# A pre-norm attention and mixture-of-experts layer on one core: five full expert tiles of the first sequence are listed while the last router blocks are still chosen, and the expert stage takes buffers in x's place

## The chip, the cores and the metric

One core of one Trainium2 chip runs the whole layer. The metric is device microseconds. Engines: PE (TensorE, matmul), DVE (VectorE), ACT (ScalarE), POOL (GpSimd), SP (which issues most DMAs); each runs its instructions in program order, and they meet at semaphores.

## The reference

```python
x = x + attn(layernorm(x))                      # (2, 2048, 256), 16 heads, softmax, then a local band is added
n = layernorm(x)
probs = softmax(gelu(n @ rW1 + rb1) @ rW2 + rb2)     # 4 experts
weights, chosen = top_k(probs, 2)
out = sum over chosen e of weights_e * (gelu(n @ We1[e] + be1[e]) @ We2[e] + be2[e])
x = x + out
```

Each of the 4096 tokens goes to two of four experts, so 8192 rows pass through an expert.

## The kernel before

After projections and attention come two functions on one block of engine programs. `route` takes the tokens in 8 blocks of 512 (four to a sequence). Per block PE gathers the attention output and the local band (`heads`), multiplies by Wo (`projection`), DVE adds the residual and normalises (`normalise`), PE transposes, ACT and DVE split the result in two float32r halves (`xT_hi`, `xT_lo`), PE makes the router's hidden layer in three products (`router`, L1219, 24 matmuls), ACT applies Gelu, PE makes the logits (L1227) and transposes them. DVE chooses the two experts (`gate`), ACT takes the exponentials, DVE weighs them. PE counts by small matmuls which slot of its expert's region each token gets (`count_slots`, L1243 to L1248), DVE turns that into row numbers (`give_slots`), and POOL scatters the rows to DRAM, eight indirect DMAs a block (`scatter`, L955). The blocks overlap: the choice for block i-1 is written behind the residual of block i+1. When the last block has its slots, DVE makes the table of tiles (`tabulate`, L1086 to L1109): for each of 19 tiles of 512 rows its first row and its expert.

`experts` runs the 19 tiles. SP loads a tile's rows, weights (two halves of 2 MB) and biases, PE transposes the rows (L1475) and ACT and DVE split them. Then per eighth `m` of the hidden layer: `hidden` (L1492, 6 matmuls), Gelu on ACT (L1392), a split on DVE (L1419, L1421), `output` (L1508, 12 matmuls). `hidden` runs two steps ahead of `output`. POOL gathers the output rows, DVE adds, POOL stores. SP waits for every scatter before it loads any tile (L1318), and tile 1's load for the table. The weights of the first tile are loaded earlier (L933), when `o` and `v` have been read, in whose place they stand.

The order is that of the code: each engine's program is written out, and nothing reorders it.

Of the kernel before, what the change touches and what calls it, by code (L numbers as in the profile page):

```python
# [20 lines left out]
F32 = mybir.dt.float32  # L21
# [8 lines left out]
P = 128  # L30
# [5 lines left out]
BT = 4  # L36
# [36 lines left out]
STEPS = TOKENS // SLOTS - 1  # L73

# [749 lines left out]
def route(nc, ctx, dram, keep, block):  # L824
# [3 lines left out]
    def sem(name):  # L828
# [74 lines left out]
    scattered, residual_out, first_weights, table_ready = (  # L903
        keep[n] for n in ("scattered", "residual_out", "first_weights", "table_ready"))
    CONSTS, SETS = 5, 1 + XROWS
    SCATTERS = PER_TOKEN * BT

    @block.sync
    def _(sp):
# [8 lines left out]
        def store_residual(i):  # L918
            sp.wait_ge(residual, i + 1)
            sp.dma_start(dram["out"].rearrange("(n p) f -> p n f", p=P)[:, i * BT:(i + 1) * BT, :],  # L920
                         x_sb[:, i * BT:(i + 1) * BT, :]).then_inc(residual_out, 16)
# [7 lines left out]
        for i in range(1, BLOCKS):  # L929
# [3 lines left out]
        sp.dma_start(keep["w"][0][:].bitcast(F32), dram["w_split"][0:W_CHUNKS].rearrange("c p s f -> p c s f")  # L933
                     ).then_inc(first_weights, 16)
        store_residual(BLOCKS - 1)

    @block.gpsimd
    def _(pool):
# [25 lines left out]
        for i in range(BLOCKS - 2, BLOCKS):  # L964
            scatter(i)

    @block.scalar
    def _(act):
# [34 lines left out]
        for i in range(3):  # L1003
            stage(i)
            copy_heads(i)
            if i == 1:
                copy_hi(0)
        for i in range(BLOCKS):
# [13 lines left out]
        exponentials(BLOCKS - 1)  # L1022

    @block.vector
    def _(dve):
# [4 lines left out]
        per_tile = [P, MOE_TILES, EXPERTS]  # L1030
# [14 lines left out]
        def gate(i):  # L1045
# [39 lines left out]
        def tabulate():  # L1085
            small(nc.vector.tensor_tensor(count[:], free_slot[:], regions, ALU.subtract))  # L1086
            small(nc.vector.tensor_tensor(over[:], count[:].unsqueeze(2).broadcast_to([P, EXPERTS, STEPS]),
                                          full_tiles.unsqueeze(1).broadcast_to([P, EXPERTS, STEPS]), ALU.is_gt))
            small(nc.vector.tensor_reduce(tiles_of[:], over[:], axis=AXIS.X, op=ALU.add))
            small(nc.vector.tensor_scalar_add(tiles_of[:], tiles_of[:], 1.0))  # L1090
            small(nc.vector.tensor_tensor(earlier[:], before[:, 1], tiles_of[:].unsqueeze(1).broadcast_to(pairwise),
                                          ALU.mult))
            small(nc.vector.tensor_reduce(first_tile[:], earlier[:], axis=AXIS.X, op=ALU.add))
            small(nc.vector.memset(reached[:], 0.0))
            small(nc.vector.tensor_tensor(reached[:, :, 0:EXPERTS], tile_at.unsqueeze(2).broadcast_to(per_tile),
                                          first_tile[:].unsqueeze(1).broadcast_to(per_tile), ALU.is_ge))
            small(nc.vector.tensor_tensor(chosen[:], reached[:, :, 0:EXPERTS], reached[:, :, 1:EXPERTS + 1],
                                          ALU.subtract))
            small(nc.vector.scalar_tensor_tensor(shift_of[:], first_tile[:], -float(SLOTS), regions, ALU.mult, ALU.add))
            small(nc.vector.tensor_tensor(by_expert[:], chosen[:], shift_of[:].unsqueeze(1).broadcast_to(per_tile),  # L1100
                                          ALU.mult))
            small(nc.vector.tensor_reduce(start_of[:], by_expert[:], axis=AXIS.X, op=ALU.add))
            small(nc.vector.tensor_tensor(start_of[:], start_of[:], tile_slots, ALU.add))
            small(nc.vector.tensor_scalar_min(start_of[:], start_of[:], float(EXPERTS * REGION)))
            small(nc.vector.tensor_copy(table[:, 0, :], start_of[:]))
            small(nc.vector.tensor_tensor(by_expert[:], chosen[:], expert_at.unsqueeze(1).broadcast_to(per_tile),
                                          ALU.mult))
            small(nc.vector.tensor_reduce(expert_of[:], by_expert[:], axis=AXIS.X, op=ALU.add))
            nc.vector.tensor_copy(table[:, 1, :], expert_of[:]).then_inc(table_ready, 1)  # L1109
# [28 lines left out]

        normalise(0)
        for i in range(BLOCKS):  # L1140
# [12 lines left out]
        read_logits(BLOCKS - 1)  # L1153
        gate(BLOCKS - 1)
        weigh(BLOCKS - 1)
        give_slots(BLOCKS - 1)
        tabulate()

    @block.tensor
    def _(pe):  # L1160
# [90 lines left out]

        heads(0)
        projection(0)
        heads(1)
        for i in range(BLOCKS):
# [18 lines left out]
def experts(nc, ctx, dram, keep, block):  # L1274
    def sb(name, shape, dt=F32):
        return ctx.enter_context(nc.sbuf_tensor(name, shape, dt))

    def sem(name):
        return ctx.enter_context(nc.semaphore(name))

    LAG, PS_H, H, HALVES = 2, 2, 2, 4
    TURN = 4
    ident, w, chosen, table = (keep[n] for n in ("ident", "w", "chosen", "table"))
    xs = [sb(f"xs{u}", [P, BT, ROW]) for u in range(2)]
    biases = [sb(f"biases{u}", [P, MH + DIM]) for u in range(2)]
    xT = [(sb(f"xT_hi{u}", [P, KD, SLOTS], F32R), sb(f"xT_lo{u}", [P, KD, SLOTS], F32R)) for u in range(2)]
    h = [sb(f"h{c}", [P, SLOTS]) for c in range(H)]
    h_hi = [sb(f"h_hi{c}", [P, SLOTS], F32R) for c in range(HALVES)]
    h_lo = [sb(f"h_lo{c}", [P, SLOTS], F32R) for c in range(HALVES)]
    gates = [sb(f"gates{u}", [P, BT, EXPERTS]) for u in range(2)]  # L1290
    gate = [sb(f"gate{u}", [P, BT]) for u in range(2)]
    token = [sb(f"token{u}", [P, BT], U32) for u in range(2)]
    rows = [sb(f"rows{u}", [P, BT, DIM]) for u in range(2)]
    y = [sb(f"y{u}", [P, BT, DIM]) for u in range(2)]
    psum = ctx.enter_context(nc.psum_tensor("psum_experts", [P, 8, BLOCK], F32))
    ps_h = [psum[:, c, :] for c in range(PS_H)]
    ps_x = psum[:, 2:4, :]
    ps_y = [psum[:, 4 + 2 * u:6 + 2 * u, :] for u in range(2)]

    scattered, residual_out, first_weights, table_ready = (  # L1300
        keep[n] for n in ("scattered", "residual_out", "first_weights", "table_ready"))
    xs_in = [sem(f"xs_in{u}") for u in range(2)]
    biases_in = [sem(f"biases_in{u}") for u in range(2)]
    w1_in = [sem(f"w1_in{u}") for u in range(2)]
    w2_in = [sem(f"w2_in{u}") for u in range(2)]
    x_tr, x_hi, x_lo = sem("x_tr"), sem("x_hi"), sem("x_lo")
    prepared, prep_step = sem("prepared"), sem("prep_step")
    h_ready, gelu_done, hi_ready, lo_ready, h_used = (
        sem(n) for n in ("h_ready", "gelu_done", "h_hi_ready", "h_lo_ready", "h_used"))
    y_read, y_gated, y_summed = (sem(n) for n in ("y_read", "y_gated", "y_summed"))  # L1310
    rows_set, gathered, out_stored = sem("rows_set"), sem("gathered"), sem("out_stored")
    W1 = W_CHUNKS // 2
    SCATTERS = PER_TOKEN * BT * BLOCKS // 2

    @block.sync
    def _(sp):
        for u in range(2):
            sp.wait_ge(scattered[u], 16 * SCATTERS)  # L1318
        for i in range(MOE_TILES):
            u = i % 2  # L1320
            if i == 0:
                start, expert = 0, 0
            else:
                sp.wait_ge(table_ready, 1)
                start = sp.value_load(table[0:1, 0, i:i + 1], min_val=0, max_val=EXPERTS * REGION)
                expert = sp.value_load(table[0:1, 1, i:i + 1], min_val=0, max_val=EXPERTS - 1)
            if i >= 2:
                sp.wait_ge(x_tr, i - 1)
                sp.wait_ge(prepared, i - 1)
            sp.dma_start(xs[u][:], dram["xs"][ds(start, SLOTS), :].rearrange("(t p) f -> p t f", p=P)  # L1330
                         ).then_inc(xs_in[u], 16)
# [315 lines left out]
```

## Time and profile before

| | |
|---|---|
| median of 3 runs | 2113.79 us (2111.5 to 2116.76) |
| profiled execution, own time | 2119.99 us |
| its span | 2118.2 us |
| PE, DVE, ACT, POOL busy | 2015.6, 1645.9, 1400.4, 394.8 us |
| mean granted clock of PE | 0.972 |

Busy time is a sum over stages that differ. Attention fills most of the span; the router stage lies at 1459 to 1654 us, the experts at 1654 to 2118 us. What a change between the last two does is read from that stretch alone. The ends of matmuls are modelled, so a result can be ready later than its row ends.

### The profile page before, as it was taken

To read this page: it belongs to the slowest core of one execution; us is meant where nothing else is said; L and a number is where in the kernel's file an instruction comes from. 1 tells how busy PE (TensorE), PEld (TensorE's weight loads), DVE (VectorE), ACT (ScalarE), POOL (GpSimd) and SP (SyncE) were. 2 spreads that over 40 slices of the span, in tenths; PEclk is the share of its full clock that TensorE was granted. 3 is DMA by queue.
4 is the path that set the end of the run, shared out by engine and by line. 5 is a ranking of instruction groups with operands and counts; after the bars stand their busy time and mean duration, and the time that the engine had idled before them with its cause. 6 is when DMAs were issued, how large, how long until landed. Compare 5 with 4: busy or idle time off the path is not lost. (4 is left out here: it accounts for less than half of the span.)

```text
span 2118.2 us, 48429 instructions
## 1 busy us (share of the span) xinstructions
PE 2015.6 (95%) x16588; PEld 1087.0 (51%) x16588; DVE 1645.9 (78%) x1986; ACT 1400.4 (66%) x2500; POOL 394.8 (19%) x463
## 2 busy tenths in 40 slices
PE   7898999999999999999999999998996699999997
PEld 4442333333333333333333333335875599999996
DVE  6586999999999999999999999960454355565564
ACT  3235888888888888888888888896553222222221
POOL 1252001000100100100100010010245233333333
PEclk9897999999999999999999999999997799999998
DMA  7924434533543543453353354321133576776671
GB/s 260 239 52 89 90 70 86 119 74 75 122 83 70 112 98 70 93 117 70 85 119 75 74 121 84 70 69 30 65 111 140 203 263 234 261 268 247 225 271 49
DMA packets 102075, 267.68 MB, mean 126 GB/s; under 512 B 22878, under 2 KB 45920, under 8 KB 95328
## 3 DMA queue, kind: packets, MB, share of 16 engines
q1 hardware_dynamic: 91632, 241.25, 43.2%
q0 software_dynamic: 10368, 25.45, 3.5%
q8 instruction: 45, 0.74, 0.2%
q14 instruction: 30, 0.25, 0.0%
HBM read 212.87 MB, written 74.20 MB: 136 GB/s over the span
## 5 line engine op out<-in xcount | busy, mean ns | idle before, releaser
L586 DVE TENSOR_REDUCE part_max<-psum_attend 128x1 f32<-128x1024 f32 x1024 | 1241.7, 1222 | 78.5 <-PE psum_attend L708 69.7
L641 ACT ACTIVATE probs<-psum_attend 128x512 f32<-128x512 f32 x2048 | 1110.4, 595 | 156.5 <-PE psum_attend L721 71.4
L721 PE MATMUL psum_attend<-score_q,score_k 50*128 50x512 f32 x2048 | 749.2, 448 | 9.4 <-DMA max_k<-qk_pieces 8.1
L708 PE MATMUL psum_attend<-max_k,max_q 48*128 48x512 f32 x2048 | 739.2, 450 | 8.7 <-PEq L1567 6.4
L733 PE MATMUL psum_attend<-probs,v_ones 128*32 128x256 f32 x8192 | 659.0, 393 | 9.0 <-ACT heads_sb L656 8.6
L721 PEld LDWEIGHTS psum_attend<-score_q,score_k 50*128 50x128 f32 x2048 | 309.4, 186 | 418.8 <-ACT probs L641 396.3
L733 PEld LDWEIGHTS psum_attend<-probs,v_ones 128*32 128x32 f32 x8192 | 162.6, 108 | 378.1 <-issue 200.4
L708 PEld LDWEIGHTS psum_attend<-max_k,max_q 48*128 48x128 f32 x2048 | 297.1, 187 | 22.7 <-issue 14.5
L1392 ACT ACTIVATE h<-psum_experts,biases 128x512 f32<-128x512 f32 x152 | 104.8, 689 | 281.8 <-PE psum_experts L1492 251.4
L1508 PE MATMUL psum_experts<-w,h_hi 128*128 128x256 f32 x1216 | 219.7, 280 | 0.0
L1508 PEld LDWEIGHTS psum_experts<-w,h_hi 128*128 128x128 f32 x1216 | 195.6, 188 | 12.5
L1492 PE MATMUL psum_experts<-xT_hi,w 128*128 128x512 f32 x608 | 192.3, 398 | 2.4 <-DVE xT_lo L1400 2.4
L1419 DVE CAST h_hi<-h 128x512 fp32r<-128x512 f32 x152 | 64.9, 427 | 148.8 <-ACT h L1392 124.3
L1508 PE MATMUL psum_experts<-w,h_lo 128*128 128x256 f32 x608 | 170.0, 280 | 0.0
L1368 POOL DMA_INDIRECT out<-y,token x76 | 77.9, 1025 | 232.4 <-DVE y L1444 215.0
L1508 PEld LDWEIGHTS psum_experts<-w,h_lo 128*128 128x128 f32 x608 | 115.5, 190 | 0.0
L547 POOL CAST shift<-neg_max 128x16 fp32r<-128x16 f32 x31 | 6.1, 198 | 577.3 <-DVE neg_max L594 577.3
L1492 PEld LDWEIGHTS psum_experts<-xT_hi,w 128*128 128x128 f32 x608 | 104.4, 190 | 16.7 <-DVE xT_lo L1400 2.8
L1421 DVE TENSOR_TENSOR h_lo<-h,h_hi 128x512 fp32r<-128x512 f32 x152 | 105.2, 692 | 5.2
L1492 PE MATMUL psum_experts<-xT_lo,w 128*128 128x512 f32 x304 | 95.8, 396 | 0.0
L1363 POOL DMA_INDIRECT rows<-out,token x76 | 78.8, 1037 | 68.1 <-DMA out<-y,token 40.8
L512 POOL COPY v_ones<-v_sb 128x256 f32<-128x256 f32 x32 | 12.7, 398 | 353.4 <-PE psum_attend L733 353.2
(152 smaller groups left out, 1302.0 us busy)
## 6 DMA issues: line engine op xcount, KB each, us to landing
w<-w_split SPq DMA_DIRECT2D x36, 2048.0 KB, 9.1
max_q<-qk_pieces SPq DMA_DIRECT2D x192, 128.0 KB, 7.4
score_k<-qk_pieces SPq DMA_DIRECT2D x192, 128.0 KB, 4.7
xs<-in_pads SPq DMA_DIRECT2D x33, 528.0 KB, 5.7
qk_pieces<-pieces SPq DMA_DIRECT2D x32, 512.0 KB, 4.7
w_split<-w_pair SPq DMA_DIRECT2D x32, 512.0 KB, 6.4
max_k<-qk_pieces SPq DMA_DIRECT2D x192, 64.0 KB, 7.6
score_q<-qk_pieces SPq DMA_DIRECT2D x192, 64.0 KB, 2.2
```

Source lines behind the costliest of these rows:

```text
L586: nc.vector.tensor_reduce(part_max[:, t, p:p + 1], ps_m[p].rearrange("q b f -> q (b f)"), axis=AXIS.X, op=ALU.max).then_inc(m_read, 1)
L641: nc.scalar.activation(probs[kb % 2][:, chunk * BLOCK:(chunk + 1) * BLOCK], bank_of(at), ACT.Exp, scale=float(HD) ** -0.5).then_inc(exp_do ...
L708: last = nc.tensor.matmul(ps_m[p][:, h, :], max_q[u][rows, t * P:(t + 1) * P], max_k[u][rows, p * BLOCK:(p + 1) * BLOCK], start=True, stop ...
L721: nc.tensor.matmul(bank_of(at), score_k[u][rows, kb * P:(kb + 1) * P], score_q[u][rows, part * BLOCK:(part + 1) * BLOCK], start=True, stop ...
L733: last = nc.tensor.matmul(ps_o[QUAD * j:QUAD * (j + 1), at:at + BLOCK // PARTS], v_ones[u][:, kb, :], probs[kb % 2][:, j * BLOCK + at:j * ...
L1363: nc.gpsimd.indirect_dma_start(rows[u][:, t, :], None, dram["out"], bass.IndirectOffsetOnAxis(ap=token[u][:, t:t + 1], axis=0), bounds_che ...
L1368: nc.gpsimd.indirect_dma_start(dram["out"], bass.IndirectOffsetOnAxis(ap=token[u][:, t:t + 1], axis=0), y[u][:, t, :], None, bounds_check= ...
L1392: nc.scalar.activation(h[m % H][:], ps_h[m % PS_H], ACT.Gelu, bias=biases[i % 2][:, m:m + 1]).then_inc(gelu_done, 1)
L1419: nc.vector.tensor_copy(h_hi[m % HALVES][:], h[m % H][:]).then_inc(hi_ready, 1)
L1421: nc.vector.tensor_tensor(h_lo[m % HALVES][:], h[m % H][:], h_hi[m % HALVES][:].bitcast(F32), ALU.subtract).then_inc(lo_ready, 1)
L1492: last = nc.tensor.matmul(ps_h[m % PS_H], w[u][:, 2 * k + m // 4, c, at:at + P], xx[:, k, :], start=j == 0, stop=j == len(terms) - 1)
L1508: last = nc.tensor.matmul(ps_y[u][:, t // 2, (t % 2) * DIM:(t % 2 + 1) * DIM], hs[m % HALVES][:, toks], w[u][:, chunk, c, at:at + DIM], st ...
```

## The change

`route` and `experts` become one function, `route_and_experts`, with one set of semaphores. Its main parts:

- Four blocks put 4096 rows into four regions, so at least five tiles are full by then. DVE lists five full tiles (`list_early`) in the loop's sixth round, and the other 14 (`list_late`) inside the first expert tile. The table is read by SP for every tile, the first included.
- SP loads tile 0 when blocks 0 to 3 have been scattered and stored and the first list stands; tile 1 follows. From tile 5 on it waits for all scatters and the second list.
- PE's transposes of tile 0 stand ahead of the last router block, two `hidden` steps around the last logits, and the last `count_slots` behind tile 0's second `output`. DVE chooses, weighs and places the last block between the steps of tile 0. POOL gathers tile 0's rows ahead of the last scatter.
- Rows, hidden values and biases of the tiles lie where blocks 0 to 3 of `x_sb` were, other buffers in place of the router's; PSUM banks are shared with the router's tensors.

```diff
+EARLY = PER_TOKEN * SEQ // SLOTS - EXPERTS + 1
+LATE = MOE_TILES - EARLY
...
+    x_at = x_sb[:].rearrange("p t f -> p (t f)")
...
+    y = [x_sb[:, HALF * BT:HALF * BT + BT, :], attnT[:].rearrange("p k (a f) -> p (k a) f", f=DIM)]
+    rows = [o_st, v_st]
...
+    LAST_LOGITS, LAST_GATES, LAST_SLOTS, LATE_TABLE = 0, 1, 3, 4
...
         sp.wait_ge(staged, BLOCKS)
-        sp.dma_start(keep["w"][0][:].bitcast(F32), dram["w_split"][0:W_CHUNKS].rearrange("c p s f -> p c s f")
-                     ).then_inc(first_weights, 16)
+        def load_tile(i):
+            u = i % 2
+            if i == 0:
+                sp.wait_ge(residual_out[0], 16 * HALF)
+                sp.wait_ge(table_ready, 1)
+                for parity in range(2):
+                    sp.wait_ge(scattered[parity], 16 * SCATTERS * ROUNDS)
+            elif i == EARLY:
+                sp.wait_ge(table_ready, 2)
+                for parity in range(2):
+                    sp.wait_ge(scattered[parity], 16 * SCATTERS * BLOCKS // 2)
...
+        load_tile(0)
         store_residual(BLOCKS - 1)
+        for i in range(1, MOE_TILES):
+            load_tile(i)
...
+        gather_rows(0)
+        scatter(BLOCKS - 1)
+        store_rows(0)
...
         for i in range(BLOCKS):
+            if i == BLOCKS - 1:
+                split_x(0)
             for m in range(MR):
...
+                gelu(i, m)
+                if i == 0 and m == LAST_GATES:
+                    exponentials(BLOCKS - 1)
...
+        def list_early():
+            count_tiles(full[:], ALU.is_ge)
+            sum_earlier(first_full[:], full[:])
+            list_tiles(first_full[:], 0, EARLY, None)
+            small(nc.vector.tensor_scalar(taken[:], first_full[:], -1.0, float(EARLY), ALU.mult, ALU.add))
+            small(nc.vector.tensor_scalar_max(taken[:], taken[:], 0.0))
+            small(nc.vector.tensor_tensor(taken[:], taken[:], full[:], ALU.min))
...
                 read_logits(i - 1)
+                split_x(0)
+                prepare(0)
             if i >= 1:
-                gate(i - 1)
+                choose(i - 1)
                 weigh(i - 1)
+            if i == HALF + 1:
+                list_early()
         give_slots(BLOCKS - 2)
...
+                elif m == LAST_LOGITS:
+                    read_logits(BLOCKS - 1)
+                elif m == LAST_GATES:
+                    choose(BLOCKS - 1)
+                elif m == LAST_SLOTS:
+                    weigh(BLOCKS - 1)
+                    give_slots(BLOCKS - 1)
+                elif m == LATE_TABLE:
+                    list_late()
...
+            if i == BLOCKS - 1:
+                tile_transposes(0)
             router(i)
         count_slots(BLOCKS - 2)
+        hidden(0, 0)
         router_logits(BLOCKS - 1)
+        hidden(0, 1)
         transpose_logits(BLOCKS - 1)
-        count_slots(BLOCKS - 1)
...
                 output(i, m)
+                if i == 0 and m == LAST_GATES:
+                    count_slots(BLOCKS - 1)
```

The order on DVE at the turn from round 5 to round 6 of the router loop, before (the last step of `weigh(4)`, the low half for block 6, then the slots of block 4):

```order
L1068 TENSOR_TENSOR prob<-prob,top 128x16 [waits gate_step]
L1069 TENSOR_TENSOR xrow<-prob,mask 128x4x4 [waits gate_step]
L1142 TENSOR_TENSOR route_xT_lo<-psum_route,route_xT_hi 128x1024 [waits hi_ready,gate_step]
L1075 TENSOR_TENSOR place<-psum_route,free_slot 128x16 [waits place_ready]
L1077 TENSOR_TENSOR free_slot<-psum_route,free_slot 128x4 [waits gate_step]
```

The same place now; the twenty rows from `count` to the third `taken` are `list_early`:

```order
L1203 TENSOR_TENSOR prob<-prob,top 128x16 [waits gate_step]
L1204 TENSOR_TENSOR xrow<-prob,mask 128x4x4 [waits gate_step]
L1249 TENSOR_TENSOR count<-free_slot,numbers 128x4 [waits gate_step]
L1250 TENSOR_TENSOR over<-count,numbers 128x28 [waits gate_step]
...
L1241 CAST table<-expert_of 128x5 [waits gate_step]
L1259 TENSOR_SCALAR taken<-first_full 128x4
L1260 TENSOR_SCALAR taken<-taken 128x4 [waits gate_step]
L1261 TENSOR_TENSOR taken<-taken,full 128x4 [waits gate_step]
L1351 TENSOR_TENSOR route_xT_lo<-psum_route,route_xT_hi 128x1024 [waits hi_ready,gate_step]
L1210 TENSOR_TENSOR place<-psum_route,free_slot 128x16 [waits place_ready]
```

The low half that PE's router matmuls of block 6 wait for now stands behind twenty more instructions of DVE.

PE behind the last router matmuls, now (`w_end` holds the high half of tile 0's rows, `rh` the router's hidden layer; before, the logits of L1461 followed the counting at once, and transposes, the last counting and only then the tile's transposes came after):

```order
L1482 MATMUL psum_route<-mask,counting 128x4 x4
L1509 MATMUL psum_route<-w_end,w 128x512 x2
L1509 MATMUL psum_route<-xT_lo,w 128x512 x2
L1509 MATMUL psum_route<-w_end,w 128x512 x2
L1461 MATMUL psum_route<-rh,w_r 32x512 x4
L1509 MATMUL psum_route<-w_end,w 128x512 x2
L1509 MATMUL psum_route<-xT_lo,w 128x512 x2
L1509 MATMUL psum_route<-w_end,w 128x512 x2
L1468 MATMUL psum_route<-ident_sb,logitsT 128x128 x4
L1509 MATMUL psum_route<-w_end,w 128x512 x2
```

Three `hidden` steps of tile 0 now stand around the last block's logits.

SP at the end of the router loop, now (before, the 4 MB of weights stood first, without a table, and waited for `staged` alone):

```order
L962 DMA out<-x_sb 128x4x256 [waits residual]
L987 TENSOR_LOAD table [waits scattered0,table_ready,scattered1,residual_out0,staged]
L987 ISA x2
L988 TENSOR_LOAD table
L988 ISA x2
L992 ISA
L992 DMA x_sb<-xs 128x4x264
L996 ISA
L996 DMA w<-w_split 128x4x1024
```

Tile 0's rows are now behind the first list, and its weights behind its rows.

## Rows read from the trace of the kernel before

**Rows 1.** Chain of waits, 1616 to 1672 us: start, duration, what

```profile
1601.24 52.92 issue
...
1654.21 3.80 DMA xs<-xs
...
1658.05 1.98 PE psum_experts L1475 x8
...
1662.39 6.69 PE psum_experts L1492 x18
1669.08 1.39 PE psum_experts L1508 x12
```

**Rows 2.** Busy time by stretch: PE, weight loads, DVE, ACT, POOL, clock, DMA, GB/s

```profile
1592.00:1598.00 6.00, 6.00 (x40) 5.25 (x36) 1.16 (x5) 3.71 (x5) 1.92 (x2) 1.00 1.03 420
...
1613.00:1619.00 6.00, 5.07 (x11) 3.57 (x12) 3.69 (x16) 0.69 (x1) 2.70 (x3) 0.50 0.18 68
...
1635.00:1658.00 23.00, 3.58 (x16) 3.49 (x16) 5.24 (x29) 0.00 (x0) 15.31 (x16) 0.50 0.35 119
...
1695.00:1717.95 22.95, 22.95 (x152) 20.88 (x151) 13.63 (x24) 6.39 (x9) 8.12 (x8) 1.00 0.70 249
```

**Rows 3.** Timeline of PE: start, duration, line, operation, count, idle time before

```profile
1592.26 0.40 PE L1243 MATMUL psum_route<-mask,counting 128*128 128x16 f32 x2
...
1594.07 3.70 PE L1191 MATMUL psum_route<-w_o,attnT 128*128 128x256 f32 x16
...
1598.82 0.72 PE L1219 MATMUL psum_route<-route_xT_hi,w_r_hi 128*128 128x512 f32 x2 [0.61 <-DVE route_xT_lo L1142]
...
1603.06 0.72 PE L1219 MATMUL psum_route<-route_xT_hi,w_r_hi 128*128 128x512 f32 x2 [2.58 <-DVE logits L1042]
...
1607.36 1.03 PE L1202 MATMUL psum_route<-ident_sb,xrow 128*128 128x128 f32 x8
...
1613.85 1.22 PE L1219 MATMUL psum_route<-route_xT_hi,w_r_hi 128*128 128x512 f32 x2 [2.03 <-DVE route_xT_lo L1142]
...
1622.25 0.29 PE L1243 MATMUL psum_route<-mask,counting 128*128 128x16 f32 x2
```

**Rows 4.** Timeline of DVE

```profile
1597.54 1.22 DVE L1142 TENSOR_TENSOR route_xT_lo<-psum_route,route_xT_hi 128x1024 fp32r<-128x1024 f32 x1
...
1599.61 1.22 DVE L1115 TENSOR_TENSOR x_sb<-psum_route,x_sb 128x1024 f32<-128x1024 f32 x1
...
1632.35 0.22 DVE L1042 TENSOR_REDUCE logits<-psum_route 128x16 f32<-128x64 f32 x1
...
1639.63 0.15 DVE L1086 TENSOR_TENSOR count<-free_slot,numbers 128x4 f32<-128x4 f32 x1
...
1643.62 0.18 DVE L1109 CAST table<-expert_of 128x19 int32<-128x19 f32 x1
```

**Rows 5.** Timeline of ACT

```profile
1628.35 0.60 ACT L1016 ACTIVATE logitsT<-psum_route 128x512 f32<-128x512 f32 x1 [5.22 <-remote]
1628.97 1.28 ACT L1001 ACT_TABLE_LOAD   x1
1630.26 0.22 ACT L1001 ACTIVATE prob<-below_top 128x16 f32<-128x16 f32 x1
```

**Rows 6.** Costliest groups: busy, mean ns of one, idle before

```profile
L1392 ACT ACTIVATE h<-psum_experts,biases 128x512 f32<-128x512 f32 x152 | 104.8, 689 | 281.8 <-PE psum_experts L1492 251.4
L1419 DVE CAST h_hi<-h 128x512 fp32r<-128x512 f32 x152 | 64.9, 427 | 148.8 <-ACT h L1392 124.3
L1421 DVE TENSOR_TENSOR h_lo<-h,h_hi 128x512 fp32r<-128x512 f32 x152 | 105.2, 692 | 5.2
```

**Rows 7.** Timeline of SP, tile 0's biases and tile 1's rows

```profile
1654.62 0.51 SPq L1346 DMA_DIRECT2D biases<-in_be  x1
1656.75 0.39 SPq L1330 DMA_DIRECT2D xs<-xs  x1
```

**Rows 8.** Timeline of POOL, the last indirect DMA of block 3

```profile
1593.55 0.96 POOL L955 DMA_INDIRECT xs<-xrow,slot_at  x1 [0.30 <-issue]
```

More of the change, by code:

```diff
@@ L821, in _, with route_and_experts @@
         transpose_heads(ps_tr).then_inc(last_tr, 1)
-def route(nc, ctx, dram, keep, block):
+def route_and_experts(nc, ctx, dram, keep, block):
     def sb(name, shape, dt=F32):
@@ new lines, in route_and_experts @@
+    LAG, PS_H, H, HALVES = 2, 2, 2, 4
+    TURN = 4
+    w = keep["w"]
+    x_at = x_sb[:].rearrange("p t f -> p (t f)")
+    ends = np.cumsum([0, BT * ROW, BT * ROW, SLOTS, SLOTS, MH + DIM, MH + DIM])
+    xs0, xs1, h0, h1, biases0, biases1 = (x_at[:, int(a):int(b)] for a, b in zip(ends, ends[1:]))
+    xs = [part.rearrange("p (t f) -> p t f", f=ROW) for part in (xs0, xs1)]
+    h, biases = [h0, h1], [biases0, biases1]
+    y = [x_sb[:, HALF * BT:HALF * BT + BT, :], attnT[:].rearrange("p k (a f) -> p (k a) f", f=DIM)]
@@ new lines, in route_and_experts @@
+    full = sb("full", [P, EXPERTS])
+    first_full = sb("first_full", [P, EXPERTS])
+    taken = sb("taken", [P, EXPERTS])
+    ps_x = psum[:, 2:4, :]
+    ps_h = [psum[:, 4 + c, :] for c in range(PS_H)]
+    ps_y = [psum[:, 6:8, :], psum[:, 0:2, :]]
+    xs_in = [sem(f"xs_in{u}") for u in range(2)]
+    biases_in = [sem(f"biases_in{u}") for u in range(2)]
+    w1_in = [sem(f"w1_in{u}") for u in range(2)]
+    w2_in = [sem(f"w2_in{u}") for u in range(2)]
+    x_tr, x_hi, x_lo = sem("x_tr"), sem("x_hi"), sem("x_lo")
@@ L1021, in _, with gelu @@
                 copy_heads(i + 3)
-        exponentials(BLOCKS - 1)
+        def gelu(i, m):
+            s = MH * i + m
+            act.wait_ge(h_ready, s + 1)
+            if s < H:
+                act.wait_ge(residual_out[0], 16 * HALF)
+            else:
+                act.wait_ge(h_lo_ready, s - H + 1)
+            nc.scalar.activation(h[m % H], ps_h[m % PS_H], ACT.Gelu, bias=biases[i % 2][:, m:m + 1]
+                                 ).then_inc(gelu_done, 1)
+        for i in range(MOE_TILES):
+            act.wait_ge(biases_in[i % 2], 16 * (i // 2 + 1))
+            for m in range(MH):
+                if m == TURN + LAG and i + 1 < MOE_TILES:
+                    split_x(i + 1)
+                gelu(i, m)
+                if i == 0 and m == LAST_GATES:
+                    exponentials(BLOCKS - 1)
     @block.vector
@@ L1250, in count_slots, with tile_transposes, hidden, output @@
             last.then_inc(place_ready, 1)
+        def tile_transposes(i):
+            u = i % 2
+            pe.wait_ge(xs_in[u], 16 * (i // 2 + 1))
+            if i == 0:
+                pe.wait_ge(residual, BLOCKS)
+            else:
+                pe.wait_ge(x_lo, i)
+            for k in range(KD):
+                for t in range(BT):
+                    last = nc.tensor.transpose(ps_x[:, k, t * P:(t + 1) * P], xs[u][:, t, k * P:(k + 1) * P], ident[:])
+            last.then_inc(x_tr, 1)
+        def hidden(i, m):
+            u, s = i % 2, MH * i + m
+            if m == 0:
+                pe.wait_ge(x_lo, i + 1)
+                pe.wait_ge(w1_in[u], 16 * (i // 2 + 1))
+            if s >= PS_H:
+                pe.wait_ge(gelu_done, s - PS_H + 1)
+            hi, lo = xT[u]
+            at = (m % 4) * P
+            terms = [(c, xx, k) for c, xx in ((0, hi), (0, lo), (1, hi)) for k in range(KD)]
+            for j, (c, xx, k) in enumerate(terms):
+                last = nc.tensor.matmul(ps_h[m % PS_H], w[u][:, 2 * k + m // 4, c, at:at + P], xx[:, k, :],
+                                        start=j == 0, stop=j == len(terms) - 1)
+            last.then_inc(h_ready, 1)
+        def output(i, m):
+            u, s = i % 2, MH * i + m
+            if m == 0:
+                pe.wait_ge(w2_in[u], 16 * (i // 2 + 1))
+                if i == 0:
+                    pe.wait_ge(lg_read, BLOCKS)
+                elif i == 1:
+                    pe.wait_ge(place_read, BLOCKS)
+                else:
+                    pe.wait_ge(y_read, i - 1)
+            pe.wait_ge(h_lo_ready, s + 1)
+            chunk, at = W1 + m // 2, (m % 2) * DIM
+            for t in range(BT):
+                toks = slice(t * P, (t + 1) * P)
+                for j, (hs, c) in enumerate(((h_hi, 0), (h_hi, 1), (h_lo, 0))):
+                    last = nc.tensor.matmul(ps_y[u][:, t // 2, (t % 2) * DIM:(t % 2 + 1) * DIM],
+                                            hs[m % HALVES][:, toks], w[u][:, chunk, c, at:at + DIM],
+                                            start=m == 0 and j == 0 and t % 2 == 0,
+                                            stop=m == MH - 1 and j == 2 and t % 2 == 1)
+            last.then_inc(h_used, 1)
         heads(0)
@@ L1519, in _ @@
                 if m == TURN and i + 1 < MOE_TILES:
-                    transposes(i + 1)
+                    tile_transposes(i + 1)
                 if m + LAG < MH:
@@ L1571, in program @@
             keep["w"] = [token_sb(f"w{u}", [P, W_CHUNKS, 2, CHUNK], F32R) for u in range(2)]
-            token_sb("o_end", [P, NHEADS * (ST + 2) * HD + (NHEADS + 1) * ST * HD - 4 * W_CHUNKS * CHUNK])
-            with nc.Block() as block:
-                for stage in (route, experts):
-                    with ExitStack() as ctx:
-                        stage(nc, ctx, dram, keep, block)
+            keep["w_end"] = token_sb("w_end", [P, NHEADS * (ST + 2) * HD + (NHEADS + 1) * ST * HD - 4 * W_CHUNKS * CHUNK], F32R)
+            with nc.Block() as block, ExitStack() as ctx:
+                route_and_experts(nc, ctx, dram, keep, block)
 def local_band():
```

435 lines of the change are left out of this document (172 added, 263 removed).

## The prediction

> **What bounds the kernel now.** I read the page's slices first: PE is busy nearly everywhere, with one hole between the router stage and the experts. The chain of waits shows what the hole is made of [rows 1]: from 1601.24 us it follows no engine for 52.92 us, until tile 0's rows are fetched at 1654.21; transposes, the split and six-matmul `hidden` steps follow, and the first `output` starts at 1669.08. From there PE runs without a gap: a tile's stretch shows PE busy for all of its 22.95 us, at full clock, with DVE busy for 13.63 and ACT for 6.39 [rows 2]. So whatever makes the first `output` start earlier moves the end by as much, unless a tile gets longer. In the 23 us before the fetch PE is busy for 3.58 [rows 2]; SP waits there for POOL's last scatters, and nothing of the experts is allowed to begin.
>
> Three smaller waits inside the router matter, because the change adds to them. In block 6 PE's router matmuls start 0.61 us late, on DVE's low half, and wait 2.58 us more for the logits of block 5; in block 7 they wait 2.03 us for the low half [rows 3]. DVE has no pause ahead of the first of these: the low half at 1597.54 follows the weighing directly [rows 4]. That DVE chain is on the path.
>
> **What goes.** All of the serial tail: the last count, placing, table, last 16 scatter issues, fetch, transposes and split with PE idle. I do not count it as a difference of idle times but rebuild the new start of the first `output`, in the old clock, from the end of the last router matmul at 1622.25 [rows 3].
>
> - Before, ACT could copy the last logits at 1628.35 [rows 5], 6.10 us after that matmul; a count of slots and the logits lie between. Now one `hidden` step lies there too: 18 such matmuls took 4.30 us at full clock, from 1603.06 to 1607.36 [rows 3], so six take 1.43. Logits are copied from 1629.8.
> - ACT must then copy (0.60), load the exponential's table (1.28), take block 6's exponentials (0.22) [rows 5], load Gelu's table (1.28 again) and run the first Gelu (0.69) [rows 6]: 4.1 us, to 1633.9. PE fills part of this with the second `hidden` step and the transposes of the logits, then waits about 2 us for that Gelu.
> - DVE splits it (0.43 and 0.69 [rows 6]) and reads the logits (0.22 [rows 4]), which free the PSUM banks that `output` writes: 1.4 us with the gaps. The first `output` can start at 1635.4.
>
> That is 33.7 us before 1669.08, and the same three `hidden` steps lie ahead of it in both kernels. The last counting is now PE work behind this point; in the stream one count takes 1594.07 - 1592.26 = 1.8 us [rows 3]. Left: 31.9 us.
>
> **What it costs.** The first list is twenty DVE instructions that each wait for the one before, straight in the chain that PE waits for in block 6. The old table's eighteen stand at a pitch of (1643.62 - 1639.63)/17 = 0.235 us, and the shortest lasts 0.15 [rows 4]: 3.0 to 4.7 us. Their operands are smaller now, 5 tiles for 19, so I take 0.21 each: 4.2 us, all of it on the path, since residual, transposes and low half of block 7 follow in the same program. Nothing later in the router absorbs it: block 7 waits for DVE too.
>
> PE then idles about 4.8 us instead of 0.61 ahead of block 6's router matmuls, and 2.6 again behind the first six. Clock: in block 7 of the old kernel PE had waited 2.03 us, and the stretch from 1613 ran at a granted 0.50, the 1.2 GHz level [rows 2, 3]; likewise the first 18 expert matmuls, after the long wait, took 6.69 us [rows 1] where 18 take 4.30 at full clock. So a fall costs 2.4 us per 18 matmuls. I charge it once for block 6; bounds are 0 and 4.8 (if its transposes and logits run slow too). Block 7's own loss is in the old times already: 24 matmuls from 1613.85 to 1622.25, 8.4 us for 5.7 [rows 3]; the 2.7 may go, as tile 0's transposes now fill that wait.
>
> The Trainium skill speaks against the change here ("TensorE: Matmul & The Clock Gate", Part 1: the throttled state is the default and activity releases it). The trace agrees with it at 1613; by that rule alone both blocks would run at the lower level, which is the upper bound just given.
>
> Around the first logits of tile 0, PE's work is broken by the 2 us wait, so some first steps may run at the lower level: 0 to 2.4 us by the same price, 1.4 taken.
>
> DVE in tile 0 carries choosing, weighing, placing and the second list, some 40 instructions at 0.235 = 9.4 us. Of a normal tile's 13.63 us three additions on the output (1.22 each, as the 128x1024 low half [rows 4]) do not exist yet. 10.0 + 9.4 is under 22.95, and `hidden` runs two steps ahead of `output`, so I cost it at nothing; in the worst place, the choice (12 instructions, 2.8 us) and two tables on ACT (2.6 us) could stall PE by up to 3 us once.
>
> SP: the first list stands at about 1601.1, reading table entries takes 1656.75 - 1654.62 - 0.51 = 1.6 us [rows 7], the fetch 3.8 [rows 1]: rows at 1606.5. PE wants them behind the transposed logits of block 6, about 1616 with the shift. Covered by 9 us. Block 3's scatter was issued by 1594.5 [rows 8], so it is not what SP waits for. First weights: rows and 2.1 MB at the 420 GB/s of [rows 2] are 6 us, at 1609 to 1610, wanted about 1628. Tile 0's other weights and biases need 2.2 MB more, 5 us; the store of block 7's residual and tile 1's loads queue behind, and their first reader is PE in the middle of tile 0. POOL's four gathers ahead of the last scatter cost it about 5 us (0.96 + 0.30 each [rows 8]); the last scatter has until tile 5's load, three tiles later. The other 14 tiles keep their work, and the tail is unchanged.
>
> These loads now run beside POOL's scatters. While 4 MB of weights moved at 420 GB/s [rows 2], POOL issued its indirect DMAs at 0.96 + 0.30 us as ever [rows 8]. The Trainium skill warns that transfers from SP and POOL share the same 16 engines and interleave ("DMA: Bandwidth & Descriptors", Issuing engines are not separate DMA queues). If that halved SP's rate, rows and first weights would be there by 1616 still, so the sum stays.
>
> Sum: 31.9 - 4.2 - 2.4 - 1.4 = 23.9 us. The profiled execution took 2119.99, so it would be 2096.1; it lies 6.2 above the median of 2113.79, and against that the forecast is 2090. Best case: 31.9 - 3.0 + 2.7 = 31.6, 2082. Worst of the same mechanism: 31.9 - 4.7 - 4.8 - 2.4 - 3.0 = 17, 2097.
>
> **Rivals.**
>
> *The clock and the stalls eat more.* If PE stays at the lower level from block 6 to tile 0's first steps, block 6 loses 4.8, the logits and counts behind it some 3 (a count alone is 1.8 at full clock), and tile 0's first 36 matmuls 4.8, with a list of 4.7 and a stall of 3: the gain is 31.9 - 20 = 12, 2102. For it: four short waits of PE in a row. Against: from 1603 to 1607 it ran at full speed right behind a wait of 2.58 us [rows 3].
>
> *Tile 0's rows come late.* Its transposes stand in PE's program ahead of the last router block, so each us late is a us lost. If the rows landed only with everything behind them in SP's queue (two tiles' rows, weights and biases and a residual block, 10.3 MB at 420 GB/s, 24 us, 1627), PE would lose 11 more: gain 13, 2101. Against it: 3.8 us for the same fetch [rows 1].
>
> *The change doesn't begin early.* If the first weights came only behind all scatters, the hole would stay: 2114, perhaps 2118 with the list. Nothing in the waits asks for that.
>
> *Slower: the buffers in x's place.* Rows, hidden values, biases and one output share the area of `x_sb`. If DVE's or ACT's accesses there ran slower, each tile would stretch once DVE passes PE's 22.95 us: from 13.63 that needs a factor of 1.7. At double, 27.3 a tile, 19 tiles lose 83 us: 2173. It decides the sign from 1.3 us a tile on (24/19). Against: DVE's addition into `x_sb` takes the same 1.22 us for 128x1024 as the split into another buffer [rows 4].
>
> **Chances.** Forecast with its bounds (2082 to 2097): 0.66. Clock and stalls (2097 to 2107): 0.15. Late rows: 0.07. More gain than my best case, if the exposed part of the list is smaller: 0.04. No effect: 0.05. Slower: 0.03. Range 2081 to 2103: it takes in both middle rivals. Measurements of this kernel tell about 0.3%, 6.3 us, from no change; faster by more: 0.92, within: 0.05, slower: 0.03.
>
> **What would show it.** From the last router matmul to the first `output` it is 46.8 us in the old trace (1669.08 - 1622.25); about 14.6 would be right, with PE waits near 2 us instead of the hole. Twenty DVE rows ahead of block 6's low half, and PE idle there near 5 us with a lower clock behind. Tile 0's transposes inside block 7's wait, without a pause on a DMA. Tiles still at 23 us. Wrong if PE waits for `xs` or `w`, if a tile grows by 1 us, or if block 6's router is not delayed by the list.

## The result, and the profile after

The changed kernel takes 2094.91 us, median of 4 runs (2084.94 to 2116.38), against 2112.64 in the same job: ratio 0.9887, 95% interval 0.9839 to 0.9936. The slowest of the four was disturbed and is left out of the ratio. Forecast: 2090, 2081 to 2103. The two profiled executions took 2119.99 and 2096.47: 23.5 us, where the sum had 23.9. The same kernel timed once more in another job (first experiment) gave 0.9851, 0.9827 to 0.9876.

PE's timeline of the changed kernel, its waits from block 6 to tile 1 and the rows that the text reads, others left out (it answers to [rows 3]; L1453 router, L1468 transposed logits, L1509 `hidden`, L1528 `output`):

```profile
1603.25 1.22 PE L1453 MATMUL psum_route<-route_xT_hi,w_r_hi 128*128 128x512 f32 x2 [4.43 <-DVE route_xT_lo L1351]
1607.49 1.22 PE L1453 MATMUL psum_route<-route_xT_hi,w_r_hi 128*128 128x512 f32 x2 [1.31 <-DVE logits L1177]
1620.18 0.72 PE L1453 MATMUL psum_route<-route_xT_hi,w_r_hi 128*128 128x512 f32 x2 [1.15 <-DVE route_xT_lo L1351]
1626.17 0.29 PE L1477 MATMUL psum_route<-mask,counting 128*128 128x16 f32 x2
1633.48 0.66 PE L1468 MATMUL psum_route<-ident_sb,logitsT 128*128 128x128 f32 x4 [1.41 <-ACT logitsT L1134]
1637.01 1.22 PE L1509 MATMUL psum_route<-w_end,w 128*128 128x512 f32 x2 [2.87 <-ACT x_sb L1148]
1639.73 0.63 PE L1528 MATMUL psum_route<-w,h_hi 128*128 128x256 f32 x2
1645.99 1.03 PE L1482 MATMUL psum_route<-mask,counting 128*128 128x4 f32 x8
1649.95 0.38 PE L1528 MATMUL psum_route<-w,h_hi 128*128 128x256 f32 x1 [0.27 <-issue]
1651.38 0.62 PE L1509 MATMUL psum_route<-xT_lo,w 128*128 128x512 f32 x2 [0.45 <-issue]
1661.63 0.50 PE L1528 MATMUL psum_route<-w,h_hi 128*128 128x256 f32 x2 [1.26 <-DVE h_lo L1321]
```

The hole of [rows 1] is gone: from the end of the last router matmuls (the next row starts at 1626.17) to the first `output` it is 13.56 us, 46.8 before. No pause on rows or weights is left; the longest waits are 4.43 us in block 6, on DVE, and 2.87 ahead of the first `output`.

Stretches of the changed kernel, as [rows 2]: block 6's router, tile 0, a steady tile.

```profile
1602.00:1610.00 8.00, 5.44 (x12) 3.85 (x13) 6.76 (x24) 0.69 (x1) 2.20 (x2) 0.50 0.69 228
1639.73:1670.11 30.38, 27.53 (x169) 24.16 (x168) 17.04 (x59) 7.82 (x11) 17.73 (x18) 0.96 0.45 154
1749.21:1772.31 23.10, 23.10 (x154) 20.92 (x153) 13.76 (x24) 6.55 (x9) 8.10 (x9) 1.00 0.71 257
```

Tile 0 takes 30.38 us for 23.10. The last count is 1.7 of the difference (1645.18 to 1646.88) and the low clock of its first steps (0.50 until 1642) about 1.1; some 4.4 us are new. They lie where two engines wait for PE, which has long finished. DVE's and ACT's timelines of the changed kernel, place and Gelu:

```profile
1654.36 0.18 DVE L1210 TENSOR_TENSOR place<-psum_route,free_slot 128x16 f32<-128x16 f32 x1 [7.45 <-remote]
```
```profile
1654.36 1.27 ACT L1148 ACTIVATE x_sb<-psum_route,x_sb 128x512 f32<-128x512 f32 x2 [9.42 <-remote]
```

The count ended at 1647.02, yet `place`, which needs nothing else, starts at 1654.36, in the same instant as a Gelu that had waited 9.42 us. "remote" says that the trace names no releaser. Ends of matmuls are modelled, so a late signal and a late result look alike here; PE's later matmuls, at any rate, start from 1646.88 on. On POOL twelve indirect transfers stand without a break from 1637.19 to 1652.5 (first and last here):

```profile
1637.19 1.06 POOL L1032 DMA_INDIRECT xs<-xrow,slot_at  x1 [6.03 <-DVE slot_at L1218]
...
1651.51 1.00 POOL L1054 DMA_INDIRECT o_st<-out,token  x1 [0.30 <-issue]
```

### The profile page after: what moved, and what is told of

Read it like the earlier page. It is cut to its first block and busy times, and to the rows that moved or that the text cites. A ratio compares the mean times of both kernels' runs of the same rounds, so it can differ in the third digit from the quotient of the medians.

```text
span 2094.7 us, 48471 instructions
## 1 busy us (share of the span) xinstructions
PE 2024.2 (97%) x16588; PEld 1083.5 (52%) x16588; DVE 1647.9 (79%) x2007; ACT 1402.4 (67%) x2502; POOL 392.9 (19%) x461
## 5 line engine op out<-in xcount | busy, mean ns | idle before, releaser
L1148 ACT ACTIVATE x_sb<-psum_route,x_sb 128x512 f32<-128x512 f32 x152 | 104.5, 689 | 287.0 <-PE psum_route L1509 243.8
L1528 PE MATMUL psum_route<-w,h_hi 128*128 128x256 f32 x1216 | 218.5, 279 | 2.4 <-DVE h_lo L1321 1.3
L1528 PEld LDWEIGHTS psum_route<-w,h_hi 128*128 128x128 f32 x1216 | 195.8, 189 | 16.6 <-issue 1.7
L1319 DVE CAST h_hi<-x_sb 128x512 fp32r<-128x512 f32 x152 | 65.3, 430 | 132.8 <-ACT x_sb L1148 115.3
L1528 PE MATMUL psum_route<-w,h_lo 128*128 128x256 f32 x608 | 169.3, 278 | 0.0
L1528 PEld LDWEIGHTS psum_route<-w,h_lo 128*128 128x128 f32 x608 | 114.7, 189 | 0.2 <-issue 0.2
L1321 DVE TENSOR_TENSOR h_lo<-x_sb,h_hi 128x512 fp32r<-128x512 f32 x152 | 105.4, 693 | 5.2
L1509 PE MATMUL psum_route<-w_end,w 128*128 128x512 f32 x320 | 102.3, 401 | 2.9 <-ACT x_sb L1148 2.9
L1509 PE MATMUL psum_route<-route_xT_hi,w 128*128 128x512 f32 x288 | 91.6, 399 | 0.0
L1032 POOL DMA_INDIRECT xs<-xrow,slot_at x64 | 62.9, 984 | 29.9 <-issue 18.1
```

The source lines that it names most:

```text
L1032: nc.gpsimd.indirect_dma_start(dram["xs"], bass.IndirectOffsetOnAxis(ap=at, axis=0), xrow[i % XROWS][:, t, :], None).then_inc(scattered[i ...
L1148: nc.scalar.activation(h[m % H], ps_h[m % PS_H], ACT.Gelu, bias=biases[i % 2][:, m:m + 1]).then_inc(gelu_done, 1)
L1319: nc.vector.tensor_copy(h_hi[m % HALVES], h[m % H]).then_inc(h_hi_ready, 1)
L1321: nc.vector.tensor_tensor(h_lo[m % HALVES], h[m % H], h_hi[m % HALVES].bitcast(F32), ALU.subtract).then_inc(h_lo_ready, 1)
L1509: last = nc.tensor.matmul(ps_h[m % PS_H], w[u][:, 2 * k + m // 4, c, at:at + P], xx[:, k, :], start=j == 0, stop=j == len(terms) - 1)
L1528: last = nc.tensor.matmul(ps_y[u][:, t // 2, (t % 2) * DIM:(t % 2 + 1) * DIM], hs[m % HALVES][:, toks], w[u][:, chunk, c, at:at + DIM], st ...
```

## The experiments

Stages are compared in us from block 0's first output projection in each profiled execution (1471.34 before, 1472.15 after). That matmul starts anywhere from 1461.9 to 1483.4 in the fourteen executions, behind instructions that no edit touches (buffers lie elsewhere in three of them): so single times say little and the stages more. The stages vary too: the nine executions that have the early list in its place reach block 6's router at 127.5 to 132.1. All are start times of rows; "place" is the time from the last count's end to `place`.

| kernel | router 6 | first `output` | place | tile 0 | end of `output` | ratio to before, interval |
|---|---|---|---|---|---|---|
| before | 127.5 | 197.6 | 0.1 | 23.0 | 632.5 | |
| changed | 131.1 | 167.6 | 7.3 | 30.4 | 608.4 | 0.9887, 0.9839-0.9936 |
| again | 131.7 | 168.5 | 7.9 | 32.5 | 611.5 | 0.9851, 0.9827-0.9876 |
| list hidden | 129.7 | 166.3 | 7.9 | 31.9 | 608.7 | 0.9875, 0.9847-0.9904 |
| gather last | 130.6 | 167.3 | 2.8 | 30.2 | 608.0 | 0.9887, 0.9861-0.9913 |
| late slots | 132.1 | 168.5 | moved | 31.3 | 610.7 | 0.9878, 0.9852-0.9904 |
| few scatters | 131.2 | 164.2 | 0.1 | 26.1 | 600.8 | 0.9843, 0.9802-0.9884 |
| late weights | 127.5 | 163.9 | 6.9 | 38.9 | 613.3 | 0.9882, 0.9830-0.9934 |
| scatters later | 129.5 | 163.7 | 0.1 | 25.8 | 606.9 | 0.9882, 0.9848-0.9915 |
| list hidden, scatters later | 127.9 | 163.6 | 0.1 | 26.9 | 616.4 | 0.9899, 0.9859-0.9939 |
| later, same places | 128.9 | 162.1 | 0.1 | 38.7 | 613.5 | 0.9916, 0.9887-0.9945 |
| list hidden, later, same places | 126.4 | 160.6 | 0.1 | 36.3 | 609.8 | 0.9900, 0.9865-0.9936 |
| shifted by 64 bytes | 129.5 | 166.0 | 7.6 | 30.4 | 613.7 | 0.9917, 0.9885-0.9948 |
| short runs | 127.7 | 160.8 | 0.6 | 25.1 | 599.7 | 0.9844, 0.9810-0.9877 |

**The changed kernel again.** No edit.

> The changed kernel itself, once more. Two theories of what ate 4 of the 29.35 us by which the first `output` comes earlier are told apart by the kernels beside it. Hold: what TensorE signals after the count of the last block and after hidden(0,4) reaches VectorE and ScalarE only when the gather of tile 0's rows on POOL has landed (7.2 us after the matmuls' end in the profiled run). Queue: VectorE's work for the last block stands between the halves of tile 0 and delays them. Both expect here 2090 to 2100 us, a ratio of 0.987 to 0.992 to the kernel before, and again a wait of VectorE's `place` of 5 to 8 us that no engine's work explains.

Tile 0 took 2.1 us more than the first time: behind the same stall the clock fell to 0.57 from 1650 to 1658. The stall repeats; whether it costs clock does not. The ratio, 0.9851, lies just below what was expected.

**The list hidden.**

```diff
                 choose(i - 1)
+                if i == HALF + 1:
+                    list_early()
                 weigh(i - 1)
-            if i == HALF + 1:
-                list_early()
```

> The early list is put between the choosing and the weighing of block 4, where VectorE waited some 8 us for the exponentials. If the list's 4.0 us stand on the path and bring the low clock behind them (18 router matmuls 6.2 us for 4.3), as the prediction has it: VectorE's low half of block 6 follows at once, the wait of 4.4 us on TensorE is gone, the router of block 6 runs at full clock, and the time is 5 to 6 us less than the changed kernel's (2089 to 2091, ratio 0.986). Rival: something else (the scatter of block 3, the last block's rows) is late next and takes the place of the list: the wait changes its name and the time falls by 1 us or less.

Block 6's router began 2.0 us earlier than in the repeated kernel, not 4, and the end of `output` shows no gain. DVE's timeline here:

```profile
1600.12 0.17 DVE L1201 TENSOR_REDUCE top<-prob 128x4 f32<-128x16 f32 x1 [5.71 <-ACT prob L1109]
...
1600.95 1.22 DVE L1351 TENSOR_TENSOR route_xT_lo<-psum_route,route_xT_hi 128x1024 fp32r<-128x1024 f32 x1
```

The list is wholly hidden (it ends at 1594.4), but now the exponentials are late: ACT's copy ahead of them waited 3.39 us with no releaser named and started at 1596.40, where POOL's eight transfers of block 3 had ended at 1596.39. That speaks for the rival, but how much of the gain went there one pair does not tell: the four kernels with the list hidden have block 6's router at 126.4 to 129.7, on average 2.3 us earlier than the nine with it in its place.

**Who holds the signals?**

```diff
-        gather_rows(0)          # gather last
         scatter(BLOCKS - 1)
+        gather_rows(0)
```
```diff
-    ... LAST_SLOTS, LATE_TABLE = 0, 1, 3, 4    # late slots
+    ... LAST_SLOTS, LATE_TABLE = 0, 1, 5, 6
```

> POOL gathers tile 0's rows behind the last block's scatter and not ahead of it, so that nothing of POOL's is under way when TensorE has counted the last block. Hold: VectorE's `place` starts within 1 us of the count's end (7.2 us in the changed kernel), hidden(0,4)'s GELU comes at once, the gaps of TensorE between 1649 and 1663 shrink from 4 us to about 1, and the time falls by 2 to 4 us, to 2091 to 2093. Queue: `place` and the GELU wait as before for what TensorE does, the gaps stay, and the time stays within 1 us (or rises, if the gathered rows now come late for the sum of tile 0).

> Weighing and slots of the last block are moved behind the halves of hidden(0,5), the late list behind those of hidden(0,6); POOL's order is as in the changed kernel. Queue: the halves of hidden(0,4) and hidden(0,5) no longer wait behind `place` and the list, TensorE's gaps of 4 us go, and the time falls by 3 to 4 us. Hold: the signal of hidden(0,4) is still held until the gather has landed, so the GELU of hidden(0,4) is as late as before; the gaps shrink by 1 us at most and the time falls by 0 to 1 us.

With the gather last, `place` came 2.8 us after the count, at 1646.65, 1.1 us behind the last transfer of block 6's scatter (1644.60 + 0.96), for 7.3. But tile 0 stayed at 30.2: the run of transfers, now 1647.95 to 1663.7, stalls PE's next steps instead (0.4 to 0.7 us "issue" each, 1658 to 1662). With DVE's late work moved, a Gelu still waited 10.67 us, until 1.9 us behind the end of POOL's twelve transfers, and tile 0 took 31.3. The queue theory falls; the hold follows POOL.

**Transfers or loads?** Few scatters issues `at = slot_at[i % 2][:, 0:1]` alone for blocks 4 to 7, so that the rows that the other seven carry are missing, and the waits count the fewer scatters. Late weights:

```diff
+            if i == 1:
+                sp.wait_ge(place_read, BLOCKS)
```

> POOL issues one of the eight scatters of each of the blocks 4 to 7 and leaves out the other seven, so those blocks' rows are missing from the late tiles; the first five tiles have all their rows. Hold (what TensorE signals is held while POOL's indirect transfers are under way): TensorE's signals after the logits of blocks 6 and 7, after the count of block 7 and after hidden(0,4) come within 0.5 us of the matmuls' end; from the first output projection of block 0 to tile 1's first `output` it takes 6 to 9 us less than in the changed kernel (198.0 and 201.0 us in its two profiled runs). Rival, the loads: what holds the signals is tile 0's and tile 1's rows and weights at some 420 GB/s, which are all still loaded; the waits stay as they are and the stretch stays within 2 us.

> Tile 1's weights are asked for only when the last block's `place` has been read (some 1654 us), so that between the landing of tile 0's weights and there only POOL's transfers are under way. Loads: `place` comes within 1 us of the count's end (7.2 and 8.1 us in the changed kernel), the GELU of hidden(0,4) is on time. Hold by POOL: `place` still comes 6 to 8 us after the count, at the end of the gather. Either way hidden(1,0) now waits 1 to 4 us for weights that take some 10 us, so the time itself says little here.

DVE's `place` with few scatters, and then with late weights:

```profile
1644.05 0.17 DVE L1215 TENSOR_TENSOR place<-psum_route,free_slot 128x16 f32<-128x16 f32 x1 [0.54 <-PE psum_route L1487]
```
```profile
1639.12 0.17 DVE L1212 TENSOR_TENSOR place<-psum_route,free_slot 128x16 f32<-128x16 f32 x1 [7.27 <-issue]
```

With few scatters tile 0 is 26.1 us (23.1, the count, and 1.3 of low clock) and PE has no gap in it; tile 1 begins 7.6 and 10.7 us earlier than in the changed kernel's two executions. With late weights SP issues nothing from 1593.43 to 1639.67, and `place`, due at 1632.2, is still 6.9 us late; from 1612 to 1639.6 POOL's transfers are all that moves but for two packets of instructions. PE has gaps without a releaser from 1637 to 1652 (up to 1.4 us each), the first two begun before SP's next load; then the clock falls (0.50 from 1652 to 1656), and tile 0 takes 38.9. So it is POOL's transfers, not the loads.

**Moving them.** Blocks 5 to 7 get slot buffers of their own (four in all).

```diff
-        scatter(BLOCKS - 2)
...
         gather_rows(0)
-        scatter(BLOCKS - 1)
+        pool.wait_ge(slot_ready, BLOCKS)
+        scatter(HALF + 1)
         store_rows(0)
         for i in range(1, MOE_TILES):
             gather_rows(i)
+            if i < 3:
+                scatter(HALF + 1 + i)
```

> The scatters of the blocks 5, 6 and 7 are moved out of the way: block 5's behind the last block's slots (four slot buffers in place of two), block 6's behind the gather of tile 1's rows, block 7's behind that of tile 2's; all work is kept. Hold: the last block's signals come at once, `place` follows the count within 1 us, TensorE's idle time and its low clock in tile 0 go in part; tile 1's first `output` comes 4 to 7 us earlier than in the changed kernel, and the time falls by as much, if the scatters hold nothing in the steady tiles. Rival: the moved scatters hold TensorE's signals where they now stand, in tiles 0 to 2, and give 3 to 5 us back there; the time is within 2 us of the changed kernel's.

> The early list in VectorE's wait for block 4's exponentials and the three late scatters moved, both at once. If the list is worth 2 us there (as between the two runs of before), and the scatters 4 to 7, the time is 6 to 9 us below the changed kernel's, 2083 to 2087 where that makes 2092. If the list's gain was lost to a hold of block 3's scatter, which stays, and the moved scatters give back what they win, it is within 2 us of the changed kernel's.

Tile 1 began 8.5 and 11.5 us earlier with the scatters later, but from there each tile took 23.45 us for 23.09 and the end won only 1.5 and 4.6. With both edits tiles 2 and 3 took 25.7 and 29.8 as well: there twelve transfers (four gathers, eight scatters) and then sixteen (four stores more) stand without a break, and PE has gaps of 0.3 to 0.9 us towards the end of both. The kernel with the scatters later has the same two runs there, no gap, and tiles of 23.45 and 23.58: such a run does not always cost. For the pace there is another suspect, the places of buffers, which the extra slot buffers had moved:

```diff
-    slot_at = [sb(f"slot_at{u}", ...) for u in range(4)]
+    slot_at = [sb(f"slot_at{u}", ...) for u in range(2)]    # the other two behind all buffers
```
```diff
+    unused = sb("unused", [P, 2 * PER_TOKEN * BT], U32)     # shifted: the changed kernel and this
```

In the first two of these three, block 6's scatter follows block 5's at once and block 7's stands behind the gather of tile 1.

> The scatters of the blocks 5 and 6 behind the last block's slots, that of block 7 behind the gather of tile 1's rows, so that no scatter stands right before a store of rows; and the two extra slot buffers stand behind all other buffers in SBUF, so that the halves h_hi and h_lo lie where they lie in the changed kernel. Where the buffers lie is what cost 0.36 us a tile in the kernel with the scatters later: then the tiles take 23.1 us again, what the scatters gain (8 us at tile 1) stays to the end, and the time is 6 to 9 us below the changed kernel's of the same chip. Rival: the scatters themselves or the later stores slow each tile: the pitch stays at 23.45 us and the time is 2 us below the changed kernel's or less.

> The same with the early list in VectorE's wait for block 4's exponentials. The list is worth 2 us at block 6's router in both earlier kernels that had it so: 8 to 11 us below the changed kernel's. Rival: a longer hold in another place takes the 2 us, and it is within 1 us of the kernel with the scatters alone.

> The changed kernel with one unused buffer of 64 bytes a partition where the two extra slot buffers stood, so that all buffers behind it lie 64 bytes further; no instruction is another. If where the buffers lie sets the pace of the `output` matmuls: a tile takes 23.45 us for 23.09 (119 ns a matmul for 115), and the time is 6 to 7 us above the changed kernel's, with the stages ahead of the tiles as they were. Rival: the pace came from what the scatters' kernel did otherwise; then the tiles take 23.09 us and the time is that of the changed kernel, 2092 to 2097.

A steady tile by stretch in the shifted kernel (for the changed one's 23.10 see above):

```profile
1832.70:1856.15 23.45, 23.45 (x154) 21.32 (x153) 13.84 (x24) 6.53 (x9) 8.31 (x8) 1.00 0.70 253
```

The places explain the pace: 23.1 with the buffers back, 23.45 from the shift alone. But sixteen scatters in a row made tile 0 38.7 and 36.3 us, and tile 2, beside twelve transfers, took 25.3 and 25.5, so neither kernel won what was expected. PE's timeline in the first of these:

```profile
1659.95 0.39 PE L1513 MATMUL psum_route<-route_xT_hi,w 128*128 128x512 f32 x1 [0.71 <-issue]
1660.67 0.48 PE L1513 MATMUL psum_route<-route_xT_hi,w 128*128 128x512 f32 x1 [0.34 <-issue]
1662.75 0.37 PE L1532 MATMUL psum_route<-w,h_hi 128*128 128x256 f32 x1 [1.59 <-issue]
...
1668.38 0.37 PE L1532 MATMUL psum_route<-w,h_lo 128*128 128x256 f32 x1 [1.73 <-issue]
```

PE stops between matmuls of one step, waiting for nothing that the trace shows, until the run of transfers ends at 1667.2; then comes the low clock (0.53 over 1667 to 1676).

**Short runs.** The previous version with the list hidden, and

```diff
+        pool.wait_ge(h_used, 6)
+        scatter(HALF + 2, [0])                  # four transfers
...
+            if i == 1:
+                scatter(HALF + 2, [1])
+            elif i in (2, 3):
+                scatter(HALF + 3, [i - 2])
```

> The early list hidden, the buffers where they were, and POOL's late scatters cut into runs with pauses between: block 5's eight behind the last block's slots, four of block 6's after six of tile 0's eight steps, four behind each of the gathers of tiles 1, 2 and 3. If what stops TensorE is the length of an unbroken run of POOL's indirect transfers (twelve in the changed kernel's tile 0, sixteen in the kernel with the scatters later, where a tile of 23 us took 38.7 and 36.3), then tile 0 takes 25 to 27 us for 30.4 to 32.5, no tile behind it over 23.6, and the end of the output matmuls, counted from block 0's output projection, comes at 598 to 603 us for 608.4 and 611.5; the time is 8 to 12 us below the changed kernel's. Rival: any scatter beside the tiles costs what it would have cost before them; then the tiles lose 5 us or more between them and the time is within 3 us of the changed kernel's.

Tile 0 by stretch:

```profile
1639.00:1664.13 25.13, 25.13 (x170) 22.89 (x169) 18.86 (x63) 8.12 (x12) 12.14 (x12) 1.00 0.29 95
```

25.1 us, without a gap, at full clock, beside runs of eight and four; `output` ends at 599.7, in the range expected, 8.7 and 11.7 us before the changed kernel's. The one tile over 23.6 is tile 4 (26.45), where tile 5's loads, now asked for from 1739.3 on, are late: a Gelu waited 8.42 us for its biases. Whole runs do not separate it: its interval overlaps both of the changed kernel's, and so does that of few scatters. What POOL's transfers cost is shown by stages of profiled executions alone; there it is plain: tile 0 takes 30.2 to 38.9 us in the nine that have twelve or more transfers in a row beside it, and 25.1 to 26.9 in the four that do not.

## Why the prediction was right, step by step

- *First `output` 14.6 us behind the last router matmul.* 13.56: right, 1.0 better.
- *Low clock 1.4 in tile 0's first steps.* 2.4, the upper bound: the six `hidden` matmuls ahead of the first `output` took 2.72 (1637.01 to 1639.73) for 1.43, within the 13.56, and 1.1 came behind it.
- *List 4.2 us, all on the path.* 3.95 (1598.02 to 1601.97), and it shows as 4.43 in PE's wait. That nothing else absorbs it was half right: taken off the path it returned 2.0, and 1.6 and 2.5 in the later pairs, about as much as executions differ.
- *Low clock 2.4 in block 6.* Its last 18 matmuls took 6.2 us for 4.3: 1.9. The upper bound drawn from the Trainium skill ("TensorE: Matmul & The Clock Gate", Part 1) did not come about: the clock was back at 1.00 from 1612.
- *Block 7's own loss may go.* It went: 24 matmuls in 6.0 us, 1620.18 to 1626.17, for 8.4. That is 2.4 us that the sum left out. It is not a property of the edit: with late slots and with the gather last the same 24 took 7.2 and 8.0. Nor are the two terms independent: where block 6's 18 ran at full clock (gather last, late weights, short runs: 4.3 us each), block 7's 24 took 7.9 to 8.0. There the fall moved from one block to the other; the sum charged it in block 6 and kept it in block 7.
- *Rows and weights in time.* Right.
- *DVE's extra work in tile 0, and POOL's transfers beside the loads, at nothing.* This is the step that failed: some 4.4 us in the changed kernel, more in the repetition. One of the prediction's own signs of being wrong, a tile that grows by 1 us, came true in tile 0. I asked whether DVE had room (17.04 of 30.38 busy: it had) and whether SP's loads slowed POOL (its transfers kept 0.96 + 0.30), but not what POOL's transfers do to PE. The "remote" in ACT's row of [rows 5], 5.22 us in the old kernel, was the hint.
- *Tiles as before.* 23.15 before, 23.09 after: 1.0 us won over 17 tiles, which the sum did not have; no run shows why.

From the traces: 33.1 at the first `output` (by its row at 1668.92; the chain of [rows 1] has 1669.08), less 3.1 for blocks 6 and 7 (list and clock, less block 7's gain), less 7.4 in tile 0, plus 1.0 and 0.4 in the other tiles: 24.0; measured to the program's end 24.3 in stage time, less 0.8 for a later start. So that 23.9 came out so closely is luck: the stalls of 4.4 us and gains that the sum lacked (2.4 in block 7, 1.0 at the first `output`, 1.0 in the tiles) cancel. The rival with clock and stalls had the mechanism (a stall in tile 0) and too high a price.

## What to carry to other kernels

Before work is moved beside another engine's, ask what that engine's transfers do to the engines that only signal each other: a wait whose releaser the trace cannot name, in step with a run of indirect transfers, is a cost that moves with them. Keep such runs short and in pauses. And measure by the stage's own start, when the code ahead of it varies more than the edit is worth, and in more than one execution: here block 6's router moved by up to 4.6 us without an edit to what it waits for.

## What the runs showed of the hardware

- In the seven executions whose last count falls late in an unbroken run of POOL's indirect transfers, what waits for PE is let go only behind the run: `place`, or with late slots the Gelu, started 0.4 to 2.0 us after its last transfer. That made `place` 6.9 to 7.9 us late where the gather followed the scatter, 2.8 where the run ended sooner, and 0.1 to 0.6 late where the count stood in no run. A run alone does not do it. In the old kernel the last count fell in the fifth of sixteen transfers (1632.71 to 1652.67), with PE nearly idle (3.58 of 23 us in [rows 2]), and DVE followed 0.1 us later:

```profile
1638.69 0.17 DVE L1075 TENSOR_TENSOR place<-psum_route,free_slot 128x16 f32<-128x16 f32 x1 [2.62 <-PE psum_route L1248]
```

- In the expert tiles PE stops between matmuls without a releaser (up to 1.73 us at a time) in or just behind runs of twelve and more, from some 10 us after their start, and in the eight that follow twelve after 1.7 us (late weights). Runs of eight by themselves gave at most one such gap beside a tile, of 0.25 us, and four stores, a pause of 2.3 us and four gathers, as in each steady tile, cost nothing that shows. With the scatters later even twelve and sixteen cost nothing. What couples POOL and PE, and when, stays open; no run here shows the path.
- The Trainium skill ("DMA: Bandwidth & Descriptors", Terms) says that POOL's path writes its descriptors to rings in SBUF. Whether that writing or the transfers themselves delay PE no run separates.
- Buffers that lie 64 bytes a partition further made each tile 0.36 us longer with the same instructions, at the same clock: 119 ns an `output` matmul for 115.
